# Second attention: norm factors on GpSimd in turns of four tiles, split over two of its gaps; the first pair of tiles alone; loops of the expert layer written out

## The chip, the cores and the metric

One core of a Trainium2 chip runs the whole program. The metric is the device time of one execution in microseconds (us). The engines are TensorE (PE; PEld is its weight load), VectorE (DVE), ScalarE (ACT), GpSimd (POOL) and SyncE (SP, which only issues transfers here).

## The reference

The input x is 4 batches of 1,024 rows of 256 numbers; a context of 77 rows per batch comes beside it. Four layers follow each other, each added to x:

```
x = x + L0_xattn(ctx, ctx, layernorm(x), mask, ...)   # 16 heads of depth 16, softmax over 77 keys
x = x + L0_ffn(layernorm(x), ...)                      # 8 experts, the best 2 per row, and a shared one
x = x + L1_xattn(layernorm(x), ctx, ctx, mask, ...)    # as the first, own mask for each batch
x = x + L1_ffn(layernorm(x), ...)                      # layernorm, 8-bit rounding, 256 -> 1024, gelu, back
```

A layernorm needs each row's mean and variance, and from them two factors: the inverse root of the variance, and minus the mean times that root.

## The kernel before

The 4,096 rows are 32 tiles of 128 rows, 8 tiles to a batch; x stays in SBUF as `sb["x"]` from start to end. There are six blocks with a barrier between them: the first keys and values (0 to 27 us), the first attention (27 to 264 us), the expert layer (264 to 552 us), the second attention (552 to 806 us) and the last layer (to the end).

**Attention.** `attention_phase` runs once per layer. It is software-pipelined over steps t, written out for every engine by `lay_out_steps`; step t holds work on tiles t-1 to t+4. ACT normalises tile t+4 with `rs` and `nm` (`norm`); PE turns it, makes queries and scores; DVE masks the scores (L835) and takes each head's largest (L842), in two halves g=0 and g=1; POOL subtracts the largest (`shift`, L557), ACT takes the exponential, PE turns the result and weighs the values, DVE divides, PE projects (`project`, L714, one per tile), and DVE adds to x. In a step, POOL's order is shift g=0, `between`, shift g=1, `bias` (L563), `behind`, `norms`. So POOL has two places with free time: one ahead of shift g=0 and one between the two shifts.

**Norm factors.** DVE takes the statistics (`early_stats`, L905, and `early_moments`); POOL makes the factors in `scaled_moments`: two short operations, a power (L149) and a product, all at the end of one step. `turns` says for which tiles, after which step, and whether for this layer's norm (`own_norm`) or for the last layer's (`mlp_norm`). In the second attention a turn covers a batch, 8 tiles; only the first covers tiles 4 to 7. `ahead(t)` says whose statistics DVE takes in step t: two tiles in steps 0 to 3, later one.

**Work at the side in the second attention.** The expert layer leaves two parts per row in `mixed`; they have to be added to x. Tiles 0 to 3 are joined at the end of the expert layer on DVE (L1666), tiles 4 to 7 in the attention by `first_results` on DVE (L892), tiles 8 to 15 by `join` on POOL (L577, two tiles a time, both parts, at the steps `JOINS`), the rest by accumulating transfers that POOL issues (`fetch`). From step 10 on, ACT and POOL prepare the last layer (`norm_x`, `offset_x`, `scale_x`, `shift_x`). Its weights are rounded at steps `SCALES` and `CLIPS` (DVE) and `ROUNDS` (ACT); at the steps `ROWS`, POOL scales rows of constants (L591 for four pieces of 512 columns).

**The expert layer.** `moe_phase` first runs 8 groups of 4 tiles: router, shared expert, and POOL's scatters of rows into `slots`. Then 23 "quads" of 512 sorted rows run through the experts: SP loads a quad, PE turns it (L1233), gate, up and down products follow, and POOL writes the result with four indirect transfers per quad (L1115). PE, ACT and DVE run groups 0 to 5 and quads' steps 1 to 20 as loops whose body is two groups or steps; addresses and waited counts there come from registers. POOL's and SP's programs have no loop. After the last quad, SP waits for POOL's transfers and loads `mixed` rows of tiles 0 to 3 (L1095) and 4 to 7 (L1097). DVE joins tiles 0 to 3, takes their statistics (L1669), and makes their factors; then comes the second attention's block.

## Time and profile before

| | us |
|---|---|
| three runs, median (lowest to highest) | 985.01 (983.52 to 988.62) |
| the profiled execution's own time | 985.17 |
| its span in the trace | 983.5 |
| PE / DVE / ACT / POOL busy | 855.2 / 758.6 / 612.8 / 546.7 |

The span is what the trace covers; the execution's own time is 1.67 us longer. Busy times are sums over stages that have different limits, so the stages are read apart: a stage is changed only by what ends last in it.

### The profile page before, as it was taken

To read this page: it belongs to the slowest core of one execution; us is meant where nothing else is said; L and a number is where in the kernel's file an instruction comes from. 1 tells how busy PE (TensorE), PEld (TensorE's weight loads), DVE (VectorE), ACT (ScalarE), POOL (GpSimd) and SP (SyncE) were. 2 spreads that over 40 slices of the span, in tenths; PEclk is the share of its full clock that TensorE was granted. 3 is DMA by queue.
4 is the path that set the end of the run, shared out by engine and by line. 5 is a ranking of instruction groups with operands and counts; after the bars stand their busy time and mean duration, and the time that the engine had idled before them with its cause. 6 is when DMAs were issued, how large, how long until landed. Compare 5 with 4: busy or idle time off the path is not lost. (4 is left out here: it accounts for less than half of the span.)

```text
span 983.5 us, 23363 instructions
## 1 busy us (share of the span) xinstructions
PE 855.2 (87%) x8493; PEld 665.1 (68%) x8508; DVE 758.6 (77%) x1670; ACT 612.8 (62%) x1125; POOL 546.7 (56%) x653
## 2 busy tenths in 40 slices
PE   5799999999588888599999379999999979999995
PEld 4577777777376676499988257777777745555563
DVE  4688887777456667488886588888888849999996
ACT  2466676765434443377773155766667649999995
POOL 3444767654125555167777087489898764444330
PEclk9899999999889999699999599999999989999997
DMA  8482799400001212356662744400000000000000
GB/s 250 68 318 80 294 357 367 195 2 2 1 35 69 79 71 77 125 180 209 217 220 97 257 123 67 65 2 3 1 3 2 2 2 12 27 28 28 28 28 27
DMA packets 49536, 98.84 MB, mean 101 GB/s; under 512 B 10016, under 2 KB 32160, under 8 KB 49440
## 3 DMA queue, kind: packets, MB, share of 16 engines
q1 hardware_dynamic: 36176, 71.79, 21.6%
q0 software_dynamic: 11648, 25.18, 8.6%
q8 instruction: 62, 1.02, 0.4%
q10 hardware_dynamic: 1616, 0.58, 0.3%
q14 instruction: 34, 0.28, 0.1%
HBM read 36.71 MB, written 60.82 MB: 99 GB/s over the span
## 5 line engine op out<-in xcount | busy, mean ns | idle before, releaser
L557 POOL TENSOR_TENSOR sm_a<-sm_a,mx_a 128x616 f32<-128x616 f32 x128 | 159.1, 1244 | 148.6 <-DVE mx_a L842 148.4
L766 ACT ACTIVATE pr_a<-sm_a 128x616 f32<-128x616 f32 x128 | 91.5, 715 | 67.4 <-POOL sm_a L557 67.4
L835 DVE TENSOR_TENSOR sm_a<-pS_a,mask 128x616 f32<-128x616 f32 x128 | 101.1, 792 | 36.7 <-PE pS_a L677 35.6
L1115 POOL DMA_INDIRECT mixed<-rep,qidx_f x92 | 89.4, 972 | 50.0 <-issue 24.1
L1109 POOL DMA_INDIRECT slots<-sx,idx_f x64 | 65.6, 1026 | 82.1 <-DVE idx_f L1509 65.1
L691 PE MATMUL pT_a<-ident,pr_a 128*128 128x128 f32 x640 | 96.8, 281 | 5.1 <-ACT rep L775 2.6
L842 DVE TENSOR_REDUCE mx_a<-sm_a 128x8 f32<-128x616 f32 x128 | 99.0, 774 | 0.0
L714 PE MATMUL pO_a<-aw,ot_a 128*128 128x256 f32 x256 | 72.8, 407 | 25.3 <-DVE ot_a L863 25.2
L677 PE MATMUL pS_a<-K,q_a 64*128 64x308 f32 x512 | 88.0, 464 | 0.0
L691 PEld LDWEIGHTS pT_a<-ident,pr_a 128*128 128x128 f32 x640 | 70.0, 141 | 24.1 <-issue 13.1
L714 PEld LDWEIGHTS pO_a<-aw,ot_a 128*128 128x128 f32 x256 | 43.5, 189 | 43.9 <-DVE ot_a L863 40.6
L666 PE MATMUL pA_a<-sx,aw 128*128 128x128 f32 x512 | 71.4, 285 | 0.9 <-ACT sx L760 0.9
L666 PEld LDWEIGHTS pA_a<-sx,aw 128*128 128x128 f32 x512 | 65.2, 200 | 3.2 <-issue 1.6
L1786 PE MATMUL pU_m<-b,dg 128*128 128x512 f32 x128 | 61.1, 600 | 0.0
L677 PEld LDWEIGHTS pS_a<-K,q_a 64*128 64x128 f32 x512 | 46.0, 194 | 20.9 <-issue 13.1
L780 ACT ACTIVATE rc_a<-pO_a 128x256 f32<-128x256 f32 x64 | 24.5, 382 | 52.8 <-PE pO_a L706 52.8
L706 PE MATMUL pO_a<-rep,V 128*32 128x128 f32 x1024 | 53.1, 279 | 1.0 <-DVE x L868 1.0
L706 PE MATMUL pO_a<-V 128*32 128x128 f32 x1024 | 52.2, 276 | 1.0 <-DVE x L868 1.0
L706 PE MATMUL pO_a<-rep,sel 128*32 128x128 f32 x1024 | 52.5, 277 | 0.0
L775 ACT ACTIVATE rep<-pT_a 128x512 f32<-128x512 f32 (+1 forms) x96 | 46.5, 518 | 8.5 <-PE pT_a L691 8.0
L856 DVE TENSOR_TENSOR pO_a<-pO_a,rc_a 128x256 f32<-128x256 f32 x64 | 27.6, 431 | 31.0 <-ACT rc_a L782 27.0
L706 PE MATMUL pO_a<-V,sel 128*32 128x128 f32 x1024 | 51.4, 273 | 0.0
(305 smaller groups left out, 2415.9 us busy)
## 6 DMA issues: line engine op xcount, KB each, us to landing
slots<-sx SPq DMA_DIRECT2D x16, 2176.0 KB, 8.7
sx<-slots SPq DMA_DIRECT2D x23, 544.0 KB
x<-x_in SPq DMA_DIRECT2D x4, 1024.0 KB, 11.0
x<-mixed POOLq DMA_DIRECT2D x4, 1024.0 KB, 9.4
out_x<-x SPq DMA_DIRECT2D x32, 128.0 KB, 1.7
rep<-gu_in SPq DMA_DIRECT2D x10, 256.0 KB, 4.2
aw<-aw_in SPq DMA_DIRECT2D x2, 1024.0 KB, 6.7
ha<-mixed SPq DMA_DIRECT2D x2, 1024.0 KB, 6.9
```

The costliest lines, as they stand in the source:

```text
L557: pool.tensor_tensor(heads, heads, mx[u][:, g, :].rearrange("p (h a) -> p h a", a=1).broadcast_to([P, HG, SK]), ALU.subtract).then_inc(shi ...
L666: mm = pe.matmul(pA[:, D + g * P:D + (g + 1) * P], aw[:, k, g * P:(g + 1) * P], xt[u][:, k * P:(k + 1) * P], start=(k == 0), stop=(k == G ...
L677: mm = pe.matmul(pS[:, 2 * g + half, 0:HS], q[u][own, g * P:(g + 1) * P], K[own, t // TB, g, :], start=True, stop=True)
L691: mm = pe.transpose(pT[:, (J * t + j) % 2, (n % 4) * P:(n % 4 + 1) * P], pr[u][:, g, c * P:(c + 1) * P], sb["ident"][:])
L706: mm = pe.matmul(pO[own, at:at + P], left, pt[u][:, g * CK + c, :], start=(g == 0 and r == 0 and what == 0), stop=(r == 1), skip_group_che ...
L714: mm = pe.matmul(pO[:, 0:D], ot[u][:, k * P:(k + 1) * P], aw[:, k, 3 * D:4 * D], start=(k == 0), stop=(k == G - 1), skip_group_check=True)
L766: act.activation(pr[u][:, g, 0:NS], sm[u][:, g, :], ACT.Exp).then_inc(exped, 1)
L835: dve.tensor_tensor(sm[u][:, g, :].rearrange("p (b h k) -> p b h k", b=2, k=SK), pS[:, 2 * g:2 * g + 2, 0:HS].rearrange("p b (h k) -> p b ...
L842: dve.tensor_reduce(mx[u][:, g, :], sm[u][:, g, :].rearrange("p (h k) -> p h k", k=SK), AX.X, ALU.max).then_inc(maxed, 1)
L1109: pool.indirect_dma_start(dram["slots"][:], bass.IndirectOffsetOnAxis(idx[:, at:at + 1], 0), rows[g % 2][:, j, :], None).then_inc(moved[g ...
L1115: pool.indirect_dma_start(dram["mixed"][:], bass.IndirectOffsetOnAxis(qidx[:, at:at + 1], 0), ys[q % 2][:, j, :], None).then_inc(out_moved ...
L1786: pe.matmul(pU[u][:, half_row], dg[u][:], sb["b1"][:, half_row], start=True, stop=False)
```

## The change

1. `scaled_moments` becomes `open_norm` (the two short operations), still at the end of step t, and `close_norm` (power and product), which runs in step t+1 behind shift g=0. This holds for both attentions.
2. In the second attention turns cover four tiles, for both norms. The last layer makes the factors of 4 tiles at its start instead of 8. One tile's statistics are taken per step (`ahead`).
3. The end of the expert layer handles tiles 0 and 1 alone (`AHEAD = 2`). Tiles 2 and 3 are joined by POOL (`second_pair`), tiles 4 to 7 too (`second_half`, in place of `first_results` on DVE). SP issues seven transfers instead of four.
4. `JOINS` moves from steps -1, 0, 1, 2 to -1, 1, 3, 5; the rounding of weights moves later, and the first units of the last layer (`UNITS`, `ROUND_X`) earlier, behind `add` in DVE's step.
5. The loops over groups and quads are written out; ACT reads a quad's weight address once instead of twice.

```diff
+def open_norm(pool, sb, tiles, v, step, to):
+    pool.tensor_scalar(v, sb["mv"][:, tiles, 1], EPS, None, ALU.add).then_inc(step, 1)
+    pool.tensor_scalar(sb[to[1]][:, tiles], sb["mv"][:, tiles, 0], -1.0, None, ALU.mult).then_inc(step, 1)
+
+def close_norm(pool, sb, tiles, v, powers, n, step, to):
     rs, nm = sb[to[0]][:, tiles], sb[to[1]][:, tiles]
-    pool.tensor_scalar(v, sb["mv"][:, tiles, 1], EPS, None, ALU.add).then_inc(step, 1)
-    pool.tensor_scalar(nm, sb["mv"][:, tiles, 0], -1.0, None, ALU.mult).then_inc(step, 1)
-    pool.wait_ge(step, 4 * n + 1)
+    pool.wait_ge(step, 4 * n + 2)
     pool.tensor_tensor(rs, v, powers, ALU.pow).then_inc(step, 1)
...
-            SCALES, CLIPS, ROUNDS = (20, 21, 22, 23), (24, 25, 26, 28), (25, 26, 29, 30)
-            UNITS, ROUND_X, JOINS = (27, 29, 30, 30), (30, 31), (-1, 0, 1, 2)
+            SCALES, CLIPS, ROUNDS = (24, 25, 28, 29), (26, 27, 30, 31), (27, 28, 31, 32)
+            UNITS, ROUND_X, JOINS = (24, 25, 26, 27), (28, 29), (-1, 1, 3, 5)
...
-            turns = [(slice(ST, TB), -1, own_norm)] + [(batch(b), TB * b - 5, own_norm) for b in range(1, B)]
-            turns += [(batch(b), TB * (b + 1) + 1, mlp_norm) for b in range(B - 1)]
+            turns = [(slice(AHEAD, ST), -3, own_norm), (slice(ST, TB), -1, own_norm)]
+            turns += [(four(n), ST * n - 5, own_norm) for n in range(TB // ST, T // ST)]
+            turns += [(four(n), ST * n + 5, mlp_norm) for n in range(T // ST - 1)]
...
-            if t == -1:
-                return list(range(ST, TB))
-            if 0 <= t < ST:
-                return [TB + 2 * t, TB + 2 * t + 1]
-            if ST < t < TB + ST:
-                first = 2 * TB + t - ST - 1
-                return [first, first + 1] if t == TB + ST - 1 else [first]
-            return [2 * TB + t - ST] if TB + ST <= t < 2 * TB + ST else []
+            if t in (-3, -1):
+                return list(range(AHEAD, ST) if t == -3 else range(ST, TB))
+            return [TB + t] if 0 <= t < T - TB else []
...
+            def second_pair():
+                own = X[:, AHEAD:ST, :]
+                pool.wait_ge(sb["y_in"][1], 16 * (ST - AHEAD + 1))
+                pool.tensor_tensor(own, own, sb["sx"][0][:, AHEAD:ST, 0:D], ALU.add).then_inc(first_joined, 1)
+                pool.wait_ge(first_joined, 1)
+                for n in range(ST - AHEAD):
+                    tile = X[:, AHEAD + n, :]
+                    pool.tensor_tensor(tile, tile, sb["rep"][n][:, ST * D:(ST + 1) * D], ALU.add).then_inc(first_joined, 1)
+
+            def second_half(a):
+                of = X[:, ST:TB, :].rearrange("p t d -> p (t d)")
+                if a == 0:
+                    pool.wait_ge(sb["y_in"][2], 16 * TOPK)
+                else:
+                    pool.wait_ge(first_joined, ST - AHEAD + 1 + a)
+                pool.tensor_tensor(of, of, sb["rep"][a][:, 0:ST * D], ALU.add).then_inc(first_joined, 1)
...
             def step(t, u, has):
                 if has(1):
                     shift(t + 1, 1 - u, 0)
+                close_norms(t)
                 if layer == 1:
                     between(t)
...
                 if layer == 1:
                     behind(t)
+                if layer == 1 and t == -3:
+                    second_pair()
+                    second_half(0)
+                if layer == 1 and t == -2:
+                    second_half(1)
...
-                norms(t)
+                open_norms(t)
...
-                if layer == 1 and t == -2:
-                    first_results()
...
-        first = slice(0, ST)
+        first = slice(0, AHEAD)
...
             for a in range(TOPK):
-                sp.dma_start(sx[a][:, :, 0:D], mixed_rows(dram, a, 0, ST)).then_inc(sb["y_in"][0], 16)
+                sp.dma_start(sx[a][:, 0:AHEAD, 0:D], mixed_rows(dram, a, 0, AHEAD)).then_inc(sb["y_in"][0], 16)
+            sp.dma_start(sx[0][:, AHEAD:ST, 0:D], mixed_rows(dram, 0, AHEAD, ST - AHEAD)).then_inc(sb["y_in"][1], 16)
+            for n in range(ST - AHEAD):
+                sp.dma_start(rep[n][:, ST * D:(ST + 1) * D].rearrange("p (j d) -> p j d", d=D),
+                             mixed_rows(dram, 1, AHEAD + n, 1)).then_inc(sb["y_in"][1], 16)
...
-            with pe.Fori(0, NG // 2 - 1) as i:
-                for u in range(2):
-                    group(2 * i + u, u)
-            group(NG - 2, 0)
+            for s in range(NG - 1):
+                group(s, s % 2)
...
-                at = act.value_load(tab_w[0:1, bass.ds(q, 1)], min_val=0, max_val=(NE - 1) * WC)
+                at = weights_at.pop(q)
```

The first place is the start of POOL's program in the second attention. The names: `pr_a` and `powers_a` are constants that it fills, `x` the rows, `ha`, `sx` and `rep` hold parts of `mixed`, `sm_a` the scores, `mx_a` their largest. Before:

```order
L551 MEMSET pr_a 128x2x24 x2
L552 MEMSET powers_a 128x8
L557 TENSOR_TENSOR sm_a<-sm_a,mx_a 128x616
L577 TENSOR_TENSOR x<-x,ha 128x512
L557 TENSOR_TENSOR sm_a<-sm_a,mx_a 128x616
L563 TENSOR_TENSOR x<-x,bo 128x256
L577 TENSOR_TENSOR x<-x,ha 128x512
L146 TENSOR_SCALAR var_a<-mv 128x4
L147 TENSOR_SCALAR nm<-mv 128x4
L149 TENSOR_TENSOR rs<-var_a,powers_a 128x4
L151 TENSOR_TENSOR nm<-nm,rs 128x4
```

Now:

```order
L545 MEMSET pr_a 128x2x24 x2
L546 MEMSET powers_a 128x8
L577 TENSOR_TENSOR x<-x,sx 128x512
L581 TENSOR_TENSOR x<-x,rep 128x256 x2
L590 TENSOR_TENSOR x<-x,rep 128x1024
L138 TENSOR_SCALAR var_a<-mv 128x2
L139 TENSOR_SCALAR nm<-mv 128x2
L146 TENSOR_TENSOR rs<-var_a,powers_a 128x2
L148 TENSOR_TENSOR nm<-nm,rs 128x2
L590 TENSOR_TENSOR x<-x,rep 128x1024
L551 TENSOR_TENSOR sm_a<-sm_a,mx_a 128x616
L571 TENSOR_TENSOR x<-x,ha 128x512
```

Five additions and one turn of two tiles now stand ahead of the first shift of scores.

The second place is DVE's program at the same point (`q_a` are the queries). Before:

```order
L881 TENSOR_SCALAR mask<-m 128x616
L883 TENSOR_SCALAR mask<-mask 128x616
L848 TENSOR_TENSOR q_a<-pA_a,bqkv 128x256
L835 TENSOR_TENSOR sm_a<-pS_a,mask 128x616 x2
L892 TENSOR_TENSOR x<-x,rep 128x1024 x2
L842 TENSOR_REDUCE mx_a<-sm_a 128x8
L905 BN_STATS early_a<-x 128x6 x4
```

Now:

```order
L906 TENSOR_SCALAR mask<-m 128x616
L908 TENSOR_SCALAR mask<-mask 128x616
L921 BN_STATS early_a<-x 128x6 x2
L926 BN_AGGR mv<-early_a 128x2 x2
L873 TENSOR_TENSOR q_a<-pA_a,bqkv 128x256
L860 TENSOR_TENSOR sm_a<-pS_a,mask 128x616 x2
L867 TENSOR_REDUCE mx_a<-sm_a 128x8
L921 BN_STATS early_a<-x 128x6 x4
```

The additions left DVE; statistics of tiles 2 and 3 stand ahead of its first queries.

The third place is POOL around step 12 of the second attention, from the shift g=1 of step 11 on (`g` and `b` are rows of constants). Before:

```order
L557 TENSOR_TENSOR sm_a<-sm_a,mx_a 128x616
L563 TENSOR_TENSOR x<-x,bo 128x256
L164 TENSOR_TENSOR ha<-ha,g 128x256
L170 TENSOR_TENSOR ha<-ha,c 128x256
L146 TENSOR_SCALAR var_a<-mv 128x8
L147 TENSOR_SCALAR nm<-mv 128x8
L149 TENSOR_TENSOR rs<-var_a,powers_a 128x8
L151 TENSOR_TENSOR nm<-nm,rs 128x8
L557 TENSOR_TENSOR sm_a<-sm_a,mx_a 128x616
L591 TENSOR_SCALAR g<-g,wsi 128x512
L160 TENSOR_TENSOR x<-x,b 128x256
L557 TENSOR_TENSOR sm_a<-sm_a,mx_a 128x616
```

Now:

```order
L551 TENSOR_TENSOR sm_a<-sm_a,mx_a 128x616
L557 TENSOR_TENSOR x<-x,bo 128x256
L161 TENSOR_TENSOR ha<-ha,g 128x256
L167 TENSOR_TENSOR ha<-ha,c 128x256
L138 TENSOR_SCALAR var_a<-mv 128x4
L139 TENSOR_SCALAR nm<-mv 128x4
L551 TENSOR_TENSOR sm_a<-sm_a,mx_a 128x616
L146 TENSOR_TENSOR rs<-var_a,powers_a 128x4
L148 TENSOR_TENSOR nm<-nm,rs 128x4
L604 TENSOR_SCALAR g<-g,wsi 128x512
L157 TENSOR_TENSOR x<-x,b 128x256
L551 TENSOR_TENSOR sm_a<-sm_a,mx_a 128x616
```

Power and product moved from ahead of shift g=0 to the gap ahead of shift g=1, where the row of constants (L591, now L604) stands too.

## Rows read from the trace of the kernel before

**Rows 1.** Windows: length, busy us by engine (instructions), PE clock, DMA share, GB/s.

```profile
410.00:530.00 120.00, 118.09 (x729) 105.71 (x728) 97.96 (x201) 87.49 (x140) 82.38 (x86) 0.98 0.59 190
553.00:790.00 237.00, 213.19 (x2925) 167.61 (x2926) 195.81 (x417) 151.49 (x310) 182.87 (x201) 0.96 0.20 46
```

**Rows 2.** Timeline of ACT, once per group: start, us, operation [idle before].

```profile
289.91 0.60 ACT L1315 ACTIVATE lg_f<-pL_f 128x512 f32<-128x512 f32 x1 [3.26 <-PE pL_f L1073]
...
366.59 0.60 ACT L1315 ACTIVATE lg_f<-pL_f 128x512 f32<-128x512 f32 x1 [3.25 <-PE pL_f L1073]
381.63 0.60 ACT L1315 ACTIVATE lg_f<-pL_f 128x512 f32<-128x512 f32 x1 [3.26 <-PE pL_f L1073]
```

**Rows 3.** Quads: line view of POOL's transfers; PE's timeline, one quad apart.

```profile
L1115 POOL DMA_INDIRECT mixed<-rep,qidx_f x92: 956/961/1671, 421.7 to 537.9; - x92
...
475.32 0.60 PE L1233 MATMUL pX_f<-ident,sx 128*128 128x128 f32 x4
...
480.40 0.60 PE L1233 MATMUL pX_f<-ident,sx 128*128 128x128 f32 x4
```

**Rows 4.** Timeline and one window between the last quad and the second attention.

```profile
540.49 0.94 SPq L1095 DMA_DIRECT2D sx<-mixed  x2
...
545.92 2.48 DVE L1666 TENSOR_TENSOR x<-x,sx 128x1024 f32<-128x1024 f32 x2 [2.58 <-DMA sx<-mixed]
548.44 1.40 DVE L1669 BATCH_NORM_STATS2 st_f<-x 128x6 f32<-128x256 f32 x4
...
552.23 0.60 ACT L754 ACTIVATE sx<-x,nm,rs 128x256 f32<-128x256 f32 x1 [1.29 <-PEq L993]
...
543.50:544.00 0.50, 0.00 (x0) 0.00 (x0) 0.00 (x0) 0.00 (x0) 0.00 (x0) 1.00 1.10 389
```

**Rows 5.** Second attention's start: timeline, then line views (ns min/median/max).

```profile
560.51 2.47 DVE L892 TENSOR_TENSOR x<-x,rep 128x1024 f32<-128x1024 f32 x2
...
563.77 1.22 POOL L557 TENSOR_TENSOR sm_a<-sm_a,mx_a 128x616 f32<-128x616 f32 x1 [10.89 <-DVE mx_a L842]
564.94 1.27 POOL L577 TENSOR_TENSOR x<-x,ha 128x512 f32<-128x512 f32 x1
...
577.11 0.75 DVE L905 BATCH_NORM_STATS2 early_a<-x 128x6 f32<-128x256 f32 x2 [1.90 <-POOL x L577]
...
L881 DVE TENSOR_SCALAR mask<-m x4: 481/882/1786, 552.2 to 599.6; 128x616 f32<-128x616 uint8 x4
...
L883 DVE TENSOR_SCALAR mask<-mask x4: 482/890/2115, 552.8 to 600.8; 128x616 f32<-128x616 f32 x4
```

**Rows 6.** Timeline of PE: projections of tiles 0, 3, 4, 11, 12, 29.

```profile
579.43 1.13 PE L714 MATMUL pO_a<-aw,ot_a 128*128 128x256 f32 x4 [1.35 <-DVE ot_a L863]
...
605.55 1.13 PE L714 MATMUL pO_a<-aw,ot_a 128*128 128x256 f32 x4 [0.81 <-DVE ot_a L863]
612.43 1.13 PE L714 MATMUL pO_a<-aw,ot_a 128*128 128x256 f32 x4 [0.28 <-DVE ot_a L863]
...
661.54 1.13 PE L714 MATMUL pO_a<-aw,ot_a 128*128 128x256 f32 x4 [0.28 <-DVE ot_a L863]
670.27 1.13 PE L714 MATMUL pO_a<-aw,ot_a 128*128 128x256 f32 x4 [0.53 <-DVE ot_a L863]
...
789.74 1.13 PE L714 MATMUL pO_a<-aw,ot_a 128*128 128x256 f32 x4 [0.53 <-DVE ot_a L863]
```

**Rows 7.** Timeline of POOL: powers of 4 and 8 tiles, and a piece of constants.

```profile
570.24 1.04 POOL L149 TENSOR_TENSOR rs<-var_a,powers_a 128x4 f32<-128x4 f32 x1
...
659.75 1.66 POOL L149 TENSOR_TENSOR rs<-var_a,powers_a 128x8 f32<-128x8 f32 x1
...
662.86 1.58 POOL L591 TENSOR_SCALAR g<-g,wsi 128x512 f32<-128x512 f32 x1
```

**Rows 8.** Timeline of PE at the second attention's end: weighing, then the projection of tile 30.

```profile
792.11 0.67 PE L706 MATMUL pO_a<-rep,V 128*32 128x128 f32 x8
...
797.30 1.13 PE L714 MATMUL pO_a<-aw,ot_a 128*128 128x256 f32 x4 [0.53 <-DVE ot_a L863]
```

91 lines of the change are left out of this document (41 added, 50 removed).

## The prediction

> **What bounds the kernel now.** I read the windows by stage first, then inside each stage the timeline of one repeating operation, because its distance shows the pace and every lost microsecond.
>
> In the expert layer's groups the distance of two copies of logits is (366.59 - 289.91) / 5 = 15.34 us while PE, ACT and DVE run as loops, and 15.04 us for group 6, which was already written out [rows 2]. In the quads PE is busy 118.09 of 120 us [rows 1] and one quad takes 5.08 us; POOL issues 92 transfers from 421.7 to 537.9 us, 1.28 us each, so 5.1 us for a quad's four [rows 3]. Both engines stand at the same pace, and POOL's program has no loop. Then comes a chain without overlap: SP issues the loads at 540.49, DVE starts to join at 545.92 and takes 2.48 us, statistics of four tiles take 1.40, and the second attention begins at 552.23 [rows 4].
>
> In the second attention the pace is that of the projections: 612.43 - 605.55 = 6.88 us a step at best. From tile 0 to 3 they take 26.12 us instead of 3 x 6.88 = 20.64, so 5.5 us are lost, and from tile 4 to 29 177.31 instead of 25 x 6.88 = 172.0, so 5.3 us are lost [rows 6]. POOL is busy 182.87 of 237 us [rows 1]; it isn't full, but it has its work in the wrong places. Its power of eight tiles takes 1.66 us [rows 7], and the step behind the turn at step 11 takes 670.27 - 661.54 = 8.73 us instead of 6.88 [rows 6]. At the start it waits 10.89 us for DVE, and later DVE waits 1.90 us for its join [rows 5].
>
> **The change, part by part.**
>
> *Groups written out.* 0.30 us for each of six groups: 1.8 us. The gain is on the path, because the last group's addresses release the scatters, the loads and the quads. Bounds: nothing, and twice that.
>
> *Quads written out.* PE's pace is that of back-to-back matmuls, and POOL's issue holds the same pace with an unchanged program [rows 3]. I take 0; what ACT saves on addresses is hidden behind POOL. [...]
>
> *First pair alone.* DVE's join halves (2.48 to about 1.25 us), the statistics too (1.40 to 0.75): 1.9 us. The two first loads carry half the bytes. A load of 2 x 0.52 MB landed 5.4 us after its issue, at a rate of 389 GB/s once it flowed [rows 4], so 0.52 MB less is 1.4 us. Sum 3.3 us. Bounds: 1.9 (the landing doesn't move, as the two loads share the engines with five others that follow) and 4.3 (transfers so small start sooner).
>
> *Start of the second attention.* POOL now does the joins that DVE did in 2.47 us [rows 5]. One half is 1,024 columns; 512 columns took 1.27 us [rows 5], so at most 2.5. Its chain from the block's start: 0.7 for its constants, 1.3 + 2 x 0.7 for the second pair, 2.5, a turn of two tiles some 1.5, 2.5: 9.9 us. Before, its first shift stood at 563.77 - 552.23 = 11.5 us. So the first shift comes 1.6 us sooner, although it waits for POOL instead of DVE. DVE's first queries come some 0.5 us later, because the statistics of tiles 2 and 3 wait for POOL ahead of them; that is covered, since POOL isn't ready earlier. Afterwards step 0 carries no join any more, and its power stands in the other gap: the 1.90 us that DVE waited for the join [rows 5] go. Together 1.6 + 1.9, less 0.2 for what other waits take over: 3.3 us up to tile 0's projection. Bounds: 0.5 (the joins run at the slow rates seen beside DVE) and 4.5.
>
> *Tiles 1 to 3.* Of the 5.5 us lost I expect 2.3 back: steps 0 to 3 have one statistic less each (0.3 to 0.4 us, 1 us in all), step 2 has no join, and a mask of tile batch 1 that takes up to 1.79 + 2.12 us against 0.48 + 0.48 at its fastest [rows 5] meets a POOL with less backlog. Bounds 0.5 and 4.
>
> *Steps 4 to 29.* A turn of four has a power of 1.04 us [rows 7]; with the product 1.3 us go into the gap between the shifts and 0.5 into the gap ahead of them, instead of 2.65 in one place. Alone, each fits. But closes fall on even steps, and so do two of the four pieces of constants, steps 12 and 14: there 1.3 + 1.58 [rows 7] + 0.7 for the offset stand in one gap. What a late second shift costs is seen at the step behind turn 11: about 2.5 us late (2.2 from the turn, 0.3 from the piece) cost 1.85, so some 0.65 are absorbed. Now the lateness is 1.7 and then 2.2 us: cost 1.1 + 1.6 = 2.7 us instead of 1.85. All else lost between tiles 4 and 29 was 5.3 - 1.85 = 3.45 us; I split it in halves, as no row here divides it: 1.7 belong to the weights' sums and rounding and stay, and 1.75 belong to the turns at 9, 17, 19 and 25 and go. Sum: 1.75 - 0.85 = 0.9 us. Bounds: -1.5 (POOL's backlog over steps 12 to 15 isn't absorbed at all) and 3.5.
>
> *End of the second attention.* The matmuls of weighing take 0.67 us for eight at 792.11 and the projection of tile 30 comes 7.56 us after that of 29 [rows 8, 6], though less work is left then than in a full step. With the rounding moved behind it I take 0.8 us. Bounds 0 and 1.5. The last layer's shorter power at its start is hidden: DVE and PE begin on tiles whose factors are ready. 0.
>
> Sum: 1.8 + 3.3 + 3.3 + 2.3 + 0.9 + 0.8 = 12.4 us. From the profiled execution's own 985.17 that gives 972.8 us; that execution stands 0.16 us above the median of the three runs, so I leave it there.
>
> **Two rules beside the rows.** On the joins that move to POOL, the slope of the rows gives at most 2.5 us for 1,024 columns. The Trainium skill (GPSIMD Engine Reference, section on elementwise cycle accounting) says that a sum of two inputs runs at about 2.6 cycles an element on GpSimd, roughly half DVE's speed, and that elementwise work belongs on VectorE; by its figure a half would take an estimated 2.2 us beside DVE's 1.24, and the start would gain 0.6 us more than I took, as POOL has nothing else to do then. It speaks against the move only where POOL is the one that is late.
>
> **The rivals.**
>
> *POOL's joins and DVE's masks collide (15%).* DVE's mask operations range from 0.48 to 2.12 us for one form [rows 5], and the long ones stand beside a POOL that works without a pause. If each of POOL's new joins holds DVE up likewise, or is held up by it, the start gains only its lower bound 0.5, tiles 1 to 3 gain 0.5 and steps 4 to 29 nothing: 1.8 + 3.3 + 0.5 + 0.5 + 0 + 0.3 = 6.4, so 978.8 us. For it: POOL's chain of 9.9 us has no slack against the statistics of tiles 4 to 7. Against: DVE's joins, which are gone, were in the same place. The Trainium skill (SBUF — State Buffer, section on two separate sides) states that VectorE and GpSimd share one pair of ports under an exclusive lock held for a whole instruction. By that rule the time would be nearer to this rival's; the trace's spread agrees.
>
> *The steady part gains fully, as the even gaps absorb the pieces (13%).* Then steps 4 to 29 give 3.5: 970.2 us. It lies inside the first one's range.
>
> *Nothing that shows (8%).* The start is set by another chain, such as PE itself, whose granted clock over the second attention is 0.96 of 2.4 GHz on the mean [rows 1], so for a part of it stands at the lower level, 1.2 GHz; then only the groups and a part of the first pair pay: about 982 us.
>
> *Slower: the written-out code isn't delivered in time (5%).* If instructions of a long straight program come to PE more slowly than those of a repeated body, the quads are the place: the DMA engines are busy 0.59 of the time there [rows 1]. To end 0.5% above, each of 23 quads must lose (12.4 + 4.9) / 23 = 0.75 us; at 1 us each the time is 985.2 - 12.4 + 23 = 995.8. Against: both attentions are written out already, and keep 6.88 us a step with more matmuls per microsecond: 2,925 in 237 us against 729 in 120 [rows 1].
>
> **How the numbers follow.** The forecast case has 59%: 972.8, own range 968.5 to 976.5. With the rivals, 8 in 10 are held by 966 to 980: below lies what gathers several upper bounds, above the case of nothing and the slower one. A measurement of this kernel can tell about 0.5%, 4.9 us, from no change. Faster by more than that (under 980.1): 59 + 13 + most of 15 = 0.87; within it 0.08; slower 0.05.
>
> **What would show it.** The group distance at 15.0 us throughout; 5.07 us per quad unchanged; DVE's join of two tiles some 3.9 us after SP's issue; about 3.3 us less from the last quad's end to the block; the first shift 10 us into the block; tile 0's projection 24 us into it instead of 27.2; steps 12 and 14 longer than 6.88 and turns at 17, 19 and 25 without trace; matmuls of weighing clearly under 0.67 at the end. I am wrong if the first shift comes no sooner than 11.5 us, if a quad takes over 5.3 us, or if POOL isn't caught up again by step 16.

## The result, and the profile after the change

| | before | changed |
|---|---|---|
| median, us (lowest to highest, runs) | 986.13 (983.52 to 991.53, 7) | 980.36 (978.50 to 985.88, 7) |
| profiled execution, us | 985.17 | 978.82 |
| its span, us | 983.5 | 977.1 |

The ratio is 0.994, with a 95% interval from 0.9917 to 0.9963: the change makes the kernel 0.6% faster, 5.8 us. The prediction said 972.8 us with a range from 966 to 980, so the time lies just above the range, and the gain is a little under half of the 12.4 us forecast. The two spans differ by 6.4 us, and the account below is made on them.

Windows of the changed kernel, columns as in [rows 1] (its second attention begins 4 us earlier, so the second window does too):

```profile
410.00:530.00 120.00, 118.08 (x728) 105.42 (x728) 98.71 (x201) 87.25 (x139) 82.88 (x86) 0.99 0.61 192
549.00:786.00 237.00, 215.82 (x3000) 170.73 (x3000) 196.57 (x422) 153.07 (x314) 203.44 (x245) 0.96 0.20 46
```

The quads are as before. In the second attention POOL is busy 203.4 us instead of 182.9, for more small turns and five joins, and yet the stage is shorter.

The timeline from the groups to the second attention (ACT's copies of logits, POOL's last transfer of the quads, SP's issue, DVE's join and statistics, ACT's first tile), against [rows 2, 4]:

```profile
290.50 0.60 ACT L1332 ACTIVATE lg_f<-pL_f 128x512 f32<-128x512 f32 x1 [3.25 <-PE pL_f L1088]
...
365.67 0.60 ACT L1332 ACTIVATE lg_f<-pL_f 128x512 f32<-128x512 f32 x1 [3.26 <-PE pL_f L1088]
380.73 0.60 ACT L1332 ACTIVATE lg_f<-pL_f 128x512 f32<-128x512 f32 x1 [3.26 <-PE pL_f L1088]
...
536.98 1.91 POOL L1134 DMA_INDIRECT mixed<-rep,qidx_f  x1 [0.30 <-issue]
540.53 0.90 SPq L1110 DMA_DIRECT2D sx<-mixed  x2
...
543.94 1.42 DVE L1682 TENSOR_TENSOR x<-x,sx 128x512 f32<-128x512 f32 x2 [2.76 <-DMA sx<-mixed]
545.39 0.75 DVE L1685 BATCH_NORM_STATS2 st_f<-x 128x6 f32<-128x256 f32 x2
...
548.39 0.60 ACT L779 ACTIVATE sx<-x,nm,rs 128x256 f32<-128x256 f32 x1 [1.29 <-PEq L1008]
```

A group takes 15.0 us throughout, as forecast. But SP issues its load at 540.53, where it did so at 540.49 before: nothing of the groups' gain has arrived. From there to the block it is 7.86 us instead of 11.74, 3.9 us less.

The second attention (statistics of tiles 2 and 3, POOL's first shift, masks of the third batch, and projections of tiles 0, 3, 4, 11, 12, 13, 14, 29, 30, 31), against [rows 5, 6]:

```profile
552.05 0.75 DVE L921 BATCH_NORM_STATS2 early_a<-x 128x6 f32<-128x256 f32 x2 [2.64 <-POOL x L581]
...
558.39 1.22 POOL L551 TENSOR_TENSOR sm_a<-sm_a,mx_a 128x616 f32<-128x616 f32 x1
573.48 0.70 PE L739 MATMUL pO_a<-aw,ot_a 128*128 128x256 f32 x2 [0.20 <-DVE ot_a L888]
...
582.89 1.10 DVE L906 TENSOR_SCALAR mask<-m 128x616 f32<-128x616 uint8 x1
584.02 0.90 DVE L908 TENSOR_SCALAR mask<-mask 128x616 f32<-128x616 f32 x1
...
597.30 1.13 PE L739 MATMUL pO_a<-aw,ot_a 128*128 128x256 f32 x4 [1.36 <-DVE ot_a L888]
604.18 1.13 PE L739 MATMUL pO_a<-aw,ot_a 128*128 128x256 f32 x4 [0.27 <-DVE ot_a L888]
...
653.15 1.13 PE L739 MATMUL pO_a<-aw,ot_a 128*128 128x256 f32 x4 [0.27 <-DVE ot_a L888]
661.20 1.13 PE L739 MATMUL pO_a<-aw,ot_a 128*128 128x256 f32 x4 [0.53 <-DVE ot_a L888]
668.07 1.13 PE L739 MATMUL pO_a<-aw,ot_a 128*128 128x256 f32 x4 [0.27 <-DVE ot_a L888]
676.68 0.48 PE L739 MATMUL pO_a<-aw,ot_a 128*128 128x256 f32 x1 [0.49 <-DVE ot_a L888]
...
780.97 1.13 PE L739 MATMUL pO_a<-aw,ot_a 128*128 128x256 f32 x4 [0.53 <-DVE ot_a L888]
787.59 1.13 PE L739 MATMUL pO_a<-aw,ot_a 128*128 128x256 f32 x4 [0.53 <-DVE ot_a L888]
793.60 1.13 PE L739 MATMUL pO_a<-aw,ot_a 128*128 128x256 f32 x4 [2.41 <-DVE ot_a L888]
```

The first shift comes 10.0 us into the block, tile 0's projection 25.1 (27.2 before). Tile 12's projection comes 8.05 us after tile 11's, and tile 14's 8.61 after tile 13's. By tile 31 the changed kernel is 9.7 us ahead (803.31 before). Its span is only 6.4 us shorter, so the last layer gives 3.4 us back. Windows there, changed kernel, then ACT's first gelu:

```profile
791.00:796.00 5.00, 1.32 (x12) 0.68 (x4) 2.32 (x6) 1.75 (x3) 0.81 (x3) 0.92 0.00 0
796.00:802.00 6.00, 5.59 (x11) 2.76 (x13) 1.51 (x3) 2.37 (x3) 2.48 (x6) 0.50 0.00 0
802.00:812.00 10.00, 8.09 (x30) 3.84 (x30) 7.26 (x14) 8.77 (x15) 5.07 (x10) 1.00 0.00 0
812.00:816.00 4.00, 4.00 (x16) 2.53 (x15) 3.88 (x6) 3.32 (x6) 1.69 (x4) 0.57 0.01 2
...
802.31 1.12 ACT L1871 ACTIVATE ge_m<-pU_m,sa 128x1024 f32<-128x1024 f32 x1 [3.78 <-PE pU_m L1810]
```

The column behind POOL is the granted clock: 0.50, the 1.2 GHz level, for six us and again at 812 us. ACT waits 3.78 us for PE's first products. Ahead of the first drop PE was busy 1.3 of 5 us. In the kernel before, the end of the second attention and the same place look so:

```profile
786.00:791.60 5.60, 4.11 (x70) 2.98 (x66) 4.50 (x12) 4.16 (x9) 5.41 (x8) 1.00 0.01 3
791.60:795.00 3.40, 3.40 (x65) 2.99 (x58) 0.38 (x2) 2.20 (x4) 3.32 (x7) 0.50 0.00 0
...
800.00:805.00 5.00, 2.03 (x40) 1.31 (x28) 1.77 (x5) 0.80 (x2) 0.68 (x2) 1.00 0.01 3
805.00:809.00 4.00, 3.10 (x8) 1.85 (x9) 2.05 (x5) 2.37 (x3) 2.89 (x6) 0.57 0.01 2
809.00:826.00 17.00, 14.98 (x67) 8.12 (x68) 12.94 (x24) 14.44 (x24) 7.54 (x15) 1.00 0.00 0
```

So the kernel before has two drops as well, both short. The first, from 791.6 to 795.0 us, lies ahead of tile 30's projection, still in the second attention; the second, from 805.2 to 808.6, is half as long as the changed kernel's first. The changed kernel has its two, 6.8 and 3.4 us, both in the last layer (the first starts 1.6 us behind tile 31's projection).

### The profile page after: what moved, and what is told of

Read it like the earlier page. It is cut to its first block and busy times, and to the rows that moved or that the text cites. A ratio compares the mean times of both kernels' runs of the same rounds, so it can differ in the third digit from the quotient of the medians.

```text
span 977.1 us, 22575 instructions
## 1 busy us (share of the span) xinstructions
PE 853.5 (87%) x8493; PEld 663.6 (68%) x8508; DVE 755.8 (77%) x1668; ACT 613.1 (63%) x1124; POOL 562.5 (58%) x690
## 5 line engine op out<-in xcount | busy, mean ns | idle before, releaser
L702 PEld LDWEIGHTS pS_a<-K,q_a 64*128 64x128 f32 x512 | 45.5, 192 | 20.6 <-issue 12.6
L785 ACT ACTIVATE sx<-pA_a 128x256 f32<-128x256 f32 x64 | 24.6, 384 | 44.8 <-PE pA_a L683 44.8
L731 PE MATMUL pO_a<-rep,sel 128*32 128x128 f32 x1024 | 51.4, 273 | 0.0
L731 PE MATMUL pO_a<-V,sel 128*32 128x128 f32 x1024 | 51.4, 273 | 0.0
```

The lines of the kernel that those rows point to most:

```text
L702: mm = pe.matmul(pS[:, 2 * g + half, 0:HS], q[u][own, g * P:(g + 1) * P], K[own, t // TB, g, :], start=True, stop=True)
L731: mm = pe.matmul(pO[own, at:at + P], left, pt[u][:, g * CK + c, :], start=(g == 0 and r == 0 and what == 0), stop=(r == 1), skip_group_che ...
```

## The experiments

The runs came in five lots, each on one chip beside the kernel before. On the chips of the first, third and fifth the kernel before takes 985 to 986 us, on those of the second and fourth 1029 to 1030; so each ratio is read against its own lot. The unchanged changed kernel ran in lots 1, 3 and 5 alone. What an edit of lots 2 and 4 gains in time over it was therefore not measured, and is read from the traces. Fills are matmuls whose results nothing reads; no kernel leaves a part of the computation out.

| kernel | lot | us | ratio to before (95%) |
|---|---|---|---|
| e1_unrolled | 2 | 1013.33 | 0.9854 (0.9829 to 0.9878) |
| e2_rows_odd | 2 | 1007.03 | 0.9792 (0.9766 to 0.9817) |
| e3_masks_later | 2 | 1013.84 | 0.9840 (0.9816 to 0.9864) |
| e4_filled | 2 | 1012.54 | 0.9835 (0.9812 to 0.9858) |
| e5_before | 3 | 986.73 | 0.9997 (0.9977 to 1.0016) |
| e6_after | 3 | 981.10 | 0.9936 (0.9913 to 0.9959) |
| e7_start_filled | 3 | 980.86 | 0.9941 (0.9920 to 0.9962) |
| e8_end_filled | 3 | 974.68 | 0.9866 (0.9841 to 0.9890) |
| e9_loops | 4 | 1023.68 | 0.9952 (0.9928 to 0.9977) |
| e10_both | 4 | 1005.62 | 0.9753 (0.9721 to 0.9786) |
| e11_halves_dve | 4 | 1009.89 | 0.9807 (0.9780 to 0.9834) |
| e12_whole_turns | 4 | 1010.71 | 0.9814 (0.9781 to 0.9847) |
| e13_before_filled | 5 | 984.22 | 0.9985 (0.9965 to 1.0005) |
| e14_after | 5 | 980.30 | 0.9947 (0.9929 to 0.9965) |
| e15_both | 5 | 973.94 | 0.9880 (0.9855 to 0.9905) |
| e16_three | 5 | 972.29 | 0.9866 (0.9838 to 0.9894) |

### The loops: e1_unrolled, e9_loops

e1 is the kernel before with `for s in range(NG - 1)` and a plain `for q` in `run_quads` in place of the loops. e9 is the changed kernel with the loops put back.

> The kernel before with only its loops over groups and quads written out; both attentions stay as they were. In the changed kernel the seven group distances fell from 108.3 us together (274.54 to 380.73 is 106.2 there), but SP's first load of the joined rows is issued at 540.53 against 540.49. Theory: the groups give 2.1 us here too, and what ate them in the changed kernel (a first attention that ended 1.2 us later, a slow transfer by POOL of 1.91 us at the quads' end) is chance of one execution; then this kernel is 1 to 2 us faster than before, ratio about 0.998. Rival: the quads' pace is POOL's and its last transfers end when they end, so that the groups' gain is always lost at the quads' end: no difference at all, and the last transfer is long again.

> The changed kernel with the loops over groups and quads put back. In all eight written-out kernels so far VectorE's first work comes at 9.5 to 9.75 us, in both profiles of the kernel before at 8.6 and 8.7, and ScalarE's table load at 5.0 to 6.4 instead of 4.2 to 4.3. Theory: the longer program costs 0.95 us at its own start, so the first work is at 8.6 to 8.7 here, and the groups take 108.3 us from the first copy of logits to the last instead of 106.2; the two nearly cancel, and the time is that of the changed kernel to 1 us above it. Rival: the late start belongs to something else in the change, and stays at 9.6; then the time is 2 us above the changed kernel's.

What e1 was expected to show is missed by far: 1.5% faster. The first guess on it, scatters that land late, is only half an answer. POOL's transfers in e9, and in e10_both, which is written out, on the same chip:

```profile
L1141 POOL DMA_INDIRECT mixed<-rep,qidx_f x92: 956/960/1159, 421.7 to 576.8; - x92
its engine sat idle before it (us, times) until:
  DVE rep L1644: 62.8, 11
```

```profile
L1137 POOL DMA_INDIRECT mixed<-rep,qidx_f x92: 956/960/2205, 422.1 to 563.3; - x92
its engine sat idle before it (us, times) until:
  DVE rep L1637: 43.9, 9
```

POOL needs 155.1 us for the 92 transfers with loops and 141.2 written out, against 116.2 in the kernel before on the first chip [rows 3]. The transfers themselves are as short as ever (960 ns at the median), POOL waits for DVE. So on these chips, from about the fourth quad on, each pair of quads has a stall, which is 1.3 us longer with loops (14.2 us a pair against 12.9). That is most of the 15.7 us between e1 and the kernel before, and of the 13.0 us between e9 and e12 (1023.68 and, written out, 1010.71 in one lot), where e9 was expected at no more than 1 us over the changed kernel. On a chip like the first neither stands in the trace. What makes the stall is not settled.

The groups measure as expected: from the first copy of logits to the last 106.4 us in e1 and 108.2 in e9. The start of the program was the second finding. DVE's first work, in the kernel before and then in the changed one (the first two traces):

```profile
8.61 0.48 DVE L360 TENSOR_SCALAR bvb_a<-ones,bqkv 128x128 f32<-128x128 f32 x2 [8.61 <-DMA aw<-aw_in]
```

```profile
9.62 0.48 DVE L357 TENSOR_SCALAR bvb_a<-ones,bqkv 128x128 f32<-128x128 f32 x2 [9.62 <-DMA aw<-aw_in]
```

In the four kernels with loops (before, e5, e9, e13) it stands at 8.40 to 8.70, in all that are written out at 9.5 to 9.8, e1 among them, whose attentions are those of before. Writing out thus costs 0.8 to 1.4 us at the program's own start, through a late landing of `aw`; e9 has the rest of the change and starts at 8.40, so the rival falls. The cost doesn't end there: the first projection of the first attention comes at 49.5 to 49.9 us in the four with loops, and at 50.1 (e1) to 53.8 in the fourteen written out. In lots 1, 3 and 5 SP's first load comes at 539.7 to 540.5 us in the three with loops and at 540.5 to 543.5 in the seven written out. So there the groups' 2 us never arrived, and writing out the loops isn't shown to gain anything on such chips (e1 and e9 ran on the others alone).

### Steps 12 and 14: e2_rows_odd, e12_whole_turns

```diff
-            ABS, TOTAL, ROWS = (4, 5, 6, 7), 8, (9, 10, 12, 13, 14, 15)
+            ABS, TOTAL, ROWS = (4, 5, 6, 7), 8, (9, 10, 13, 15, 17, 19)
```

> The changed kernel with the four scalings of g2 and c2 at steps 13, 15, 17, 19 instead of 12, 13, 14, 15, so that no piece shares a gap with a power. Theory of the prediction: steps 12 and 14 took 8.05 and 8.61 us (tile 11 to 12, 13 to 14) instead of 6.88, 2.9 us in all, because close and piece met; then both are at 6.88 here and the time is 2 to 3 us under the changed kernel's, some 0.991 of before. Rival: the pieces cost the same wherever they stand, since POOL has no time left in any step: the distances move to steps 13 to 20 and the sum stays.

Tile 11's and tile 12's projection:

```profile
683.72 0.48 PE L739 MATMUL pO_a<-aw,ot_a 128*128 128x256 f32 x1 [0.28 <-DVE ot_a L888]
690.60 0.70 PE L739 MATMUL pO_a<-aw,ot_a 128*128 128x256 f32 x2 [0.27 <-DVE ot_a L888]
```

6.88 us, as at every step up to 15; from tile 11 to 16 it is 34.4 us instead of 37.4. The 3.0 us are back: a piece costs on the steps in which a turn is closed, and not on others. e12 runs `close_norms(t)` behind `open_norms(t)`, with `t == turn` in place of `t == turn + 1`:

> The changed kernel with power and product again at the end of the step that opens the turn, ahead of the next step's first shift; the turns still cover four tiles. Theory: a whole turn of four, 1.8 us, in one gap is absorbed but for 0.1 to 0.3 us at each of the 13 turns, and the pieces of constants at steps 12 and 14 meet no power any more; so steps 12 and 14 take 7.0 to 7.5 us instead of 8.05 and 8.6, and the time is 0 to 2 us under the changed kernel's. Rival: the split is what makes the turns free; each turn then costs 0.4 us or more, and the time is 2 us or more above.

The theory was right on the turns (0.1 us each), but on steps 12 and 14 both answers were wrong. Tile 12 comes after 8.17 us and tile 14 after 8.73, so the pieces collide with the whole turn nearly alike (8.05 and 8.61 with the split), and each turn costs only 0.1 us more. So it isn't the shared gap that makes them collide. The split over two gaps is worth some 0.5 us in all. What else made the turns cheap, their size or their places, these runs don't divide.

### The start of the second attention: e11_halves_dve, e7_start_filled, e3_masks_later

e11 moves `second_half(0)` and `second_half(1)` from POOL to DVE, at the end of its step -2.

> The changed kernel with the joins of tiles 4 to 7 back on VectorE, at the end of its step -2. In the changed kernel POOL's two take 2.34 and 2.36 us, and its first shift comes 10.0 us into the block. Theory: TensorE at half its clock and VectorE's chain behind it set the start together with POOL; VectorE's 2.5 us of joins stand behind the masks of tile 0, and tile 0's projection comes 25.5 to 27 us into the block instead of 24.8 to 25.1, so the move to POOL was worth 0.5 to 2 us. Rival: POOL is the one that is late, and without the joins the first shift comes 7.6 us into the block and the projection at some 23 us.

The first shift comes 12.2 us into the block and tile 0's projection 27.3, against 10.0 and 24.8 to 25.1. The move to POOL is worth 2.2 us up to there, somewhat above the theory's range; the rival, POOL as the late one, falls. By tile 3 nothing is left of it in this lot: e11 is there after 51.1 us, and e9, e10 and e12 after 51.3 to 51.4. What they lose in between is told with e7.

e7 fills TensorE's idle time there:

```diff
+            pe.wait_ge(s_bo, 2)
+            for n in range(8):
+                pe.matmul(pX[:], sb["ident"][:], aw[:, 0, 0:512], start=True, stop=True)
...
+                if layer == 1 and t in (-2, -1):
+                    for n in range(t + 3):
+                        pe.matmul(pT[:, 0, :], sb["ident"][:], aw[:, 0, 0:512], start=True, stop=True)
```

> The changed kernel with matmuls whose results nothing reads in TensorE's idle time at the start of the second attention: eight behind the last product of the expert layer (idle from 540.3 to 549.05 us), one ahead of the turn of tile 1, two ahead of the turn of tile 2. Theory: the start gained 2.1 us up to tile 0's projection instead of the 3.3 predicted, because TensorE stands at 0.5 of its clock until 567 us, and queries and scores take 2.07 and 2.42 us instead of 1.06 and 1.31; with the clock kept up, the projection comes 22 to 23.5 us after the block's start instead of 25.1, and the time falls by 1.5 to 3 us. Rival: POOL's chain (first shift 10.0 us into the block) sets the start, and the projection comes at 25 us again.

Windows of e7:

```profile
542.00:562.00 20.00, 14.78 (x59) 7.54 (x58) 10.41 (x32) 3.47 (x8) 11.02 (x14) 1.00 0.89 289
...
579.00:582.90 3.90, 1.81 (x17) 1.57 (x15) 3.83 (x10) 1.90 (x5) 0.74 (x1) 1.00 0.40 63
582.00:590.00 8.00, 6.07 (x46) 4.03 (x50) 6.73 (x16) 2.19 (x4) 4.71 (x4) 0.57 0.09 11
```

The clock stays up where it was down, and the projection comes 24.1 us into the block, some 1.0 sooner. But the block itself begins late: the eight fills end at 549.87 us, behind VectorE's chain, and from SP's first load to the projection it is 33.2 us, against 32.8 in e6. So the fills gained nothing at the start.

Then tiles 1 and 2 take 9.7 and 9.6 us instead of 7.9 and 8.0, and tile 3 comes 51.4 us into the block, 2.5 to 2.7 later than without fills. Tile 1 is late by a mask operation of VectorE, which ends right behind a row of POOL's operations:

```profile
575.72 3.35 DVE L909 TENSOR_SCALAR mask<-m 128x616 f32<-128x616 uint8 x1
...
577.12 1.60 POOL L571 TENSOR_TENSOR x<-x,ha 128x512 f32<-128x512 f32 x1
```

It takes 3.35 us instead of 1.10. TensorE, which waits, is busy for only 1.8 us of the 3.9 up to 582.9 us; its clock is down from there to 589.7 us, and tile 2 is late at that clock. The same mask operation takes 3.1 to 3.35 us in e3, e4, e9, e10 and e12, and 1.10 in the eight other traces with the change. In those with the long one it ends 0.35 us behind the last operation of an unbroken row of POOL's, tile 0's projection comes 23.9 to 24.1 us into the block, somewhat sooner than in the others, and tile 3 comes late (50.0 to 51.4 us against 48.6 to 49.1; e11 and e16, which differ there, left out). What decides between the two is not shown. e7's time is that of e6 all the same, because its second drop in the last layer is absent: from tile 31's projection to the end it takes 181.4 us instead of 184.8.

e3 has the masks of the third and fourth batch in steps 11 and 19:

```diff
-                if layer == 1 and 0 < t < B:
-                    mask_of(t)
+                if layer == 1 and t in (1, 11, 19):
+                    mask_of(1 + (1, 11, 19).index(t))
```

> The changed kernel with the masks of the third and fourth batch made in steps 11 and 19 instead of 2 and 3. In steps 1 to 3 of the changed kernel each projection comes 7.9 to 8.0 us after the one before, and VectorE has no idle time there; two mask operations of 1.10 and 0.90 us stand in each. Theory: VectorE is the bound of these three steps, so tiles 2 and 3 come at 6.9 to 7.1 us, 2 us sooner, and steps 11 and 19 hide most of a mask in VectorE's idle time: 1 to 2 us under the changed kernel. Rival: VectorE is as full in steps 11 and 19, and what is gained ahead is lost there; no difference.

Tile 3 comes 6.88 us after tile 2, so VectorE and its masks are what bounds these steps. Tile 2 should have come as soon and took 9.75 us at the lower clock, after a mask operation of 3.33 us had made tile 1 late, as in e7; e16 shows both at 6.88. And tile 11 takes 8.30 us and tile 19 8.10: a whole mask, 1.4 and 1.2 us, isn't hidden there. The rival holds, and the way out is a smaller piece (e16).

### The last layer's start: e4_filled, e8_end_filled, e13_before_filled

e8, with e4's numbers of matmuls being 4, 2 and 4:

```diff
+                if layer == 1 and t in (T - 1, T):
+                    for n in range(2 if t < T else 1):
+                        pe.matmul(pS[:, 0, :], sb["ident"][:], aw[:, 0, 0:512], start=True, stop=True)
...
             def step(t, u, has):
+                if t == -1:
+                    for n in range(2):
+                        pe.matmul(pY[:], sb["ident"][:], sb["b1"][:, 0:512], start=True, stop=True)
```

> The changed kernel with matmuls whose results nothing reads, in TensorE's idle time around the start of the last layer: four behind the weighing of tile 31, two behind its projection, four ahead of the first turn of the last layer. In the changed kernel the granted clock is 0.50 from 795.4 to 802.0 and again from 812.4 to 815.7 us, and the last layer takes 183.5 us from tile 31's projection, against 180.2 before. Theory: the drops follow TensorE's idle stretches of 2.4 and 1.5 us, and both go when these are filled; the first gelu comes 4.6 us or less into the block instead of 6.1, and the time falls by some 3 us. Rival: the clock falls there whatever TensorE does; then the same dips stand in the profile, and the time is that of the changed kernel or up to 1 us above.

> The changed kernel with the fills at the last layer's start cut to the idle time: two matmuls behind the weighing of tile 31, one behind its projection, two ahead of the first turn of the last layer. With twice as many the first gelu came 3.5 us after the block's start instead of 6.1, and the clock stayed up in the last layer, but tile 31's projection came 8.7 us after tile 30's instead of 6.0 and the first turn was late by a microsecond. Theory: idle stretches of TensorE bring the clock down; now nothing is late, and the time from tile 29's projection to the end, 196.1 us in the changed kernel and 193.8 before, falls to some 193 us: 3 us under the changed kernel. Rival: the clock falls without regard to these fills, and 196 us stay.

> The kernel before with the same small fills around the last layer's start as in e8_end_filled. From tile 31's projection to the end the kernel before takes 180.1 us with two dips of the clock of 3 us; the filled changed kernel took 178.9. Theory: the dips are in both kernels, only shorter in the one before, so the fills give it 1 to 2 us, against 6 in the changed kernel; ratio to before 0.998. Rival: the fills help both alike, 5 to 6 us, and the dips have nothing to do with the change.

In e4 the fills were twice too long (four took 3.7 us in an idle time of 2.4), so tile 31 and the first turn came late. A part of tile 31's 2.7 us isn't theirs: the clock was down from 821.8 to 825.2 us, ahead of the fills, and such a drop alone cost 1.3 us in e15. In the last layer the clock held. In e8 nothing is late. Its windows, and its first gelu:

```profile
793.00:798.00 5.00, 4.51 (x46) 2.41 (x37) 1.73 (x5) 1.75 (x3) 1.51 (x4) 1.00 0.00 0
798.00:804.00 6.00, 5.35 (x18) 2.31 (x18) 2.45 (x8) 3.95 (x6) 3.56 (x8) 1.00 0.00 0
804.00:828.00 24.00, 23.14 (x115) 13.43 (x114) 22.05 (x40) 22.30 (x36) 10.38 (x20) 1.00 0.04 12
...
802.41 1.11 ACT L1877 ACTIVATE ge_m<-pU_m,sa 128x1024 f32<-128x1024 f32 x1 [1.13 <-PE pU_m L1813]
```

The first gelu comes 6.1 us after tile 31's projection instead of 8.7, and from that projection to the end it is 178.8 us, where e6 in the same lot needs 184.8. The kernel is 6.4 us faster than e6 (974.68 against 981.10). So the drop of the clock follows TensorE's idle time here, and costs the changed kernel at least what the last layer lost. All traces agree: the five with fills there in the changed kernel (e4, e8, e10, e15, e16) have no drop from tile 31's projection until 950 us or later, and all nine without them have one of 6.8 us that begins within 2 us of it.

The Trainium skill (TensorE: Matmul & The Clock Gate, part 1 on the clock gate) states that half rate is the state at rest, which activity releases. The end of the second attention agrees, and so does the drop in e7, with TensorE busy 1.8 of the 3.9 us ahead of it. It is less plain for the first drop of the kernel before, where TensorE was busy 4.1 of the 5.6 us ahead.

In the kernel before, the same fills give 0.15% with an interval that reaches over 1. In the trace both drops are gone. Tile 30's projection comes 6.4 us after tile 29's instead of 7.56, but that isn't the fills' work, as the first of them runs 3.5 us behind it:

```profile
795.89 1.13 PE L714 MATMUL pO_a<-aw,ot_a 128*128 128x256 f32 x4 [0.53 <-DVE ot_a L866]
...
799.42 1.98 PE L745 MATMUL pS_a<-aw,ident 128*128 128x512 f32 x4
```

In the last layer nothing is gained (180.6 us from tile 31's projection to the end, 180.1 and 180.2 without). So the rival, that the fills help both kernels alike, falls. But the long drop doesn't belong to the changed kernel alone. e1, whose second attention is that of before, has no drop at tile 30 and a long one behind tile 31, and takes 182.0 us from there to the end:

```profile
828.70:835.60 6.90, 5.29 (x11) 3.10 (x12) 2.64 (x7) 2.37 (x3) 3.00 (x6) 0.51 0.00 1
```

With no drop in either, the changed kernel needs 191.4 us from tile 29's projection to the end (e8) and the kernel before 192.9 (e13).

### Repeats, and the version that beats both: e5, e6, e14, e10, e15, e16

> The kernel before, unchanged, for a trace of it beside the others of this call. On the first chip its span was 983.5 us; on the chip of the last call its time was 1028.99, and the same source with loops written out took 1013.33, 15.7 us less, where the groups can explain 2.1. Theory: on such a chip the landing of POOL's scatters sets the quads' pace (VectorE waits for it before every second quad), and the loops' waits or register arithmetic stand behind it; the quads then take clearly longer here than in the written-out kernel, about 0.6 us a quad. Rival: the first attention or another stage differs by chip, and the quads do not.

> The changed kernel, unchanged, for a second trace. If the dips of the granted clock around the last layer's start (795.4 to 802.0 and 812.4 to 815.7 us) belong to the kernel, they stand here at the same places of the program, and the last layer takes 183.5 us from tile 31's projection; if they are chance of one execution, it takes 180 to 184. Time 5 to 6 us under the kernel before on a chip like the first; on one like that of the last call some 20 us under it.

> The changed kernel, unchanged, a third trace and the comparison for the next two. If the longer dips belong to it, 183 to 185 us from tile 31's projection to the end again; if each execution draws anew, anything from 180 to 185. Ratio to before 0.994 on a chip like the first, some 0.982 on one where the scatters land late.

From tile 31's projection to the end the kernel before takes 180.2 and 180.1 us, the changed kernel 183.5, 184.8 and 183.5, with both drops at the same places of the program each time, so it repeats for the unchanged program. e7 and e9, which differ from it in other places, have the long drop alone and take 181.4 us. e5's quads have no stall on this chip, so e5 tells nothing of the other chips'. e6 is 3 us late from its first block on, where the clock was down from 22 to 26 us.

> The changed kernel with both edits that helped: g2 and c2 scaled at steps 13, 15, 17, 19 (steps 12 and 14 then took 6.88 us each, 3.0 us less together), and the small fills at the last layer's start (5.9 us less from tile 31's projection to the end). Theory: the two are in different stages and add up, 9 us under the changed kernel, ratio to before some 0.985 on a chip like the first. Rival: the granted clock depends on what the stage before did, and the steadier attention brings other dips; then the sum is 6 us or less.

> The kernel of e10_both again, beside the changed kernel on one chip. Theory: the 3.0 us of steps 12 and 14 and the 4 to 6 us of the last layer add up: 7 to 9 us under the changed kernel. Rival: less than 6, as dips come elsewhere instead.

e10's trace has steps 12 and 14 at 6.88 us each and 178.1 us from tile 31's projection to the end, so both edits do their part there. It also has a short drop ahead of tile 30, whose projection takes 7.47 us, and the long mask operation at tile 1; the sum in time couldn't be measured on that chip.

e15 is 6.4 us under e14 (973.94 against 980.30): 3.0 from steps 12 and 14 and 5.1 from the last layer, less 1.3, as a drop of the clock now falls on tile 31 (7.35 us instead of 6.01). Theory and rival met in the middle. e16 splits the masks:

```diff
+                if layer == 1 and t == 1:
+                    mask_of(1)
+                for b, first in ((2, 10), (3, 20)):
+                    if layer == 1 and t in (first, first + 1):
+                        mask_part(b, t - first)
```

> e15_both with the masks of the third and fourth batch made in steps 10 and 11, and 20 and 21, one of the two operations in each, instead of both in step 2 and in step 3. Theory: VectorE is the bound of steps 1 to 3, so two of the three distances of 7.96 us fall to 6.88, and half a mask (0.5 to 1.1 us) fits into VectorE's idle time of a later step: 1.5 to 2 us under e15_both. Rival: each half costs what it takes, as the whole one did in e3_masks_later (8.30 us instead of 6.88 at tile 11, 8.10 at tile 19), and nothing is gained.

Projections of tiles 1, 2 and 3:

```profile
580.58 0.70 PE L739 MATMUL pO_a<-aw,ot_a 128*128 128x256 f32 x2 [1.30 <-DVE ot_a L891]
587.46 0.92 PE L739 MATMUL pO_a<-aw,ot_a 128*128 128x256 f32 x3 [0.27 <-DVE ot_a L891]
594.33 0.92 PE L739 MATMUL pO_a<-aw,ot_a 128*128 128x256 f32 x3 [0.27 <-DVE ot_a L891]
```

2.2 us gained there; the halves cost 0.39, 0.50, 0.42 and 0.15 us where they now stand. Counted from tile 0's projection, e16's trace is 0.9 us ahead of e15's at tile 30, and its last layer takes 0.9 us longer again. The times differ by 1.65 us, with intervals that overlap, so a gain of e16 over e15 isn't shown. Its median is the lowest of all: 972.29 us, 1.3% under the kernel before and 0.8% under the changed one.

## Why the prediction was right and wrong

In us gained, each from the two first traces:

| term | predicted | measured |
|---|---|---|
| groups written out, as far as SP's first load | 1.8 | 0.0 |
| first pair alone | 3.3 | 3.9 |
| block's start to tile 0's projection | 3.3 | 2.1 |
| tiles 1 to 3 | 2.3 | 2.3 |
| tiles 4 to 29 | 0.9 | 0.5 |
| tiles 30 and 31 | 0.8 | 0.9 |
| last layer | 0 | -3.4 |
| sum (rounded once) | 12.4 | 6.4 |

**The step that failed most** is "The last layer's shorter power at its start is hidden ... 0". It was read for dependencies alone, and those are as said. But the clock was left out, and the last layer took 183.5 us instead of 180.15, with 10.2 us at the lower clock at its start instead of 3.4. e8 shows that this costs it: with the idle stretches filled the last layer takes 178.8 us. By e8 and e13 the change without any drop would have gained an estimated 1.5 us from tile 29 on. Why the drops fall where they do in each kernel is open: the idle stretches of 2.4 and 1.5 us stand in both kernels, and e1 has the long drop without the change in the attention.

**Tiles 30 and 31** came out as forecast (0.9 for 0.8) by luck. The matmuls of weighing at 792.11 us took 0.67 us for eight, and tile 30 7.56, because the clock was down from 791.6 to 795.0 us. In e13 and e1, where it wasn't, they need 0.40 and tile 30 6.4 us, with the rounding where it was before. The changed kernel, at full clock, needs 6.6. The gain is the drop that moved, and not the rounding.

**The groups** gain what was said (106.2 us from the first copy to the last against 108.3, even 2.1). "The gain is on the path" failed: the first attention's first projection comes 0.9 us later after the late start (the late first work belongs to the written-out code, as e1 and e9 show, but e1's first projection is only 0.3 us late), its last takes 0.3 us longer at the low clock, 0.6 are lost between the first copy of a quad's rows and POOL's first transfer, and POOL's last transfer took 1.91 us instead of 0.96; the quads gave 0.4 and the step ahead of them 0.2. The long last transfer comes and goes: it stands in e8, e13 and e14 too, not in e6. A start cost of longer code was in no rival. The rival that named the code put it at the quads and with the wrong sign for some chips. What makes the longer code late at its start is open.

**First pair alone**: mechanism right, with the landing under-sized. It gave 2.0 us instead of 1.4 (3.4 us from issue to join); DVE's two operations gave 1.7 instead of 1.9. In the second and fourth lot the join doesn't wait for the load. It follows VectorE's own copies of values (in e12 the last one starts at 572.88 us and takes 0.82, the join starts at 573.62), and from SP's issue to the block it is 11.3 to 12.6 us in all but e4, with 12.05 in e1. There this part of the change gave little or nothing that shows.

**The start**: the first shift is as worked out (10.0 us for 9.9; the join of 1,024 columns 2.34 and 2.36 for "at most 2.5"), and e11 gives 2.2 us to the move. Mis-sized is the wait of 1.90 us that was to go in full; only 0.6 us came behind the first shift. TensorE stood at 1.2 GHz until 567 us, so that its queries and scores took about twice their time; this window shows it:

```profile
549.00:567.00 18.00, 14.04 (x56) 10.10 (x56) 9.62 (x24) 5.36 (x10) 16.59 (x20) 0.51 0.99 345
```

The kernel before stood at 1.2 GHz as well, until 17.5 us into its block (18.1 in the changed one), so the clock is no difference between the two. That it took the rest isn't shown either, since e7 with the clock up gained nothing from SP's load to the projection. The Trainium skill (GPSIMD Engine Reference, section on elementwise cycle accounting) gave an estimated 2.2 us for a join; the trace has 2.35.

**Tiles 1 to 3 and 4 to 29**: right in size on this chip, the latter within 0.4 us. All of the 2.3 us stand at tile 1 (7.90 us for 10.19), where the two mask operations take 2.0 us instead of 3.9: of the reasons named, the mask beside POOL's backlog was the large one. Where the mask met that row of POOL's operations again, as in e9, e10 and e12, tiles 0 to 3 took 27.3 us, more than in the kernel before (26.1), and the term is lost. Steps 12 and 14 cost 2.9 us for a predicted 2.7, and e2 takes them away. That the split of a turn matters was overrated, as e12 shows: a piece collides with a whole turn in the other gap nearly as much. The place of the cost was right, and its reason, that piece and power share a gap, was not.

**The rivals.** "POOL's joins and DVE's masks collide" gave 978.8 us and is close in the sum, but by the wrong way: its 6 us were to be lost in the second attention, and that stage kept them. Its mechanism is in the traces all the same: mask operations take 1.10 us beside a busy POOL instead of 0.48, and up to 3.35 us in six of the fourteen traces with the change. The Trainium skill's exclusive lock on the shared ports (SBUF — State Buffer, section on two separate sides) fits that; no run here takes it apart from other causes.

## What to carry to other kernels

A gain in one stage has to be followed through every stage up to the end, and the granted clock is one of the things that it can move: compare the clock row by row in the stages that the change doesn't touch. A few unread matmuls in TensorE's idle stretches ahead of a dense stage were worth about as much here (6.4 us in e8, 5.1 from tile 31 on in e15) as the change itself (5.8), but they must be shorter than the stretch, and at the other end of the same stage they gave nothing. A term that comes out as forecast can still be luck: look at the clock of both kernels before the length of a matmul is put down to the work beside it. Work at the side costs less in pieces: the four single mask operations of e16 cost 1.5 us where they stand, the two whole masks of e3 2.6. Neither was free.

## What was not expected of the hardware

- The written-out program's first load lands about 1 us later (first use at 9.5 to 9.8 us instead of 8.4 to 8.7).
- On the chips of the second and fourth lot the quads took 12.9 us a pair written out and 14.2 us with loops, where the others take 10.1. What the stall waits for is not named by the trace.
- One mask operation takes 0.48, 1.10 or 3.35 us (VectorE, 128x616). In the six traces with the longest, and in the four with the attention of before, the masks of tile 1's step end 0.35 us behind an unbroken row of POOL's operations.
- Where drops of the clock fall isn't fixed by the stage that they fall in: one code for the last layer took 183.5 to 184.8 us in the unchanged program and 181.4 in e7 and e9, whose edits lie elsewhere.
